# Where the first layer's q, k and v projections stand, and in which order three queues serve the first phases

## The reference, cut to what matters

```
x = x + L0_attn(layernorm(x))    # Q = rope(x Wq), K = rope(x Wk), causal; softmax of (QK + 0.1 Q^2 K^2)/sqrt(8);
                                 # a second one of the half-rotated Q, K has equal scores; gate_w on out1*out2; Wo
x = x + L0_ffn(layernorm(x))     # relu(x W1 + b1) W2 + b2, 512 wide
x = x + L1_attn(layernorm(x))    # g, b, biases on q, k, v; softmax over all positions; no output projection
x = x + L1_ffn(layernorm(x))     # (silu(x Wg) * (x Wu)) Wd, int weights / 127, 384 wide
```

## Time and profile before

| | |
|---|---|
| median of 3 runs | 368.12 us |
| profiled execution | 369.26 us |
| its span, first to last instruction | 367.5 us |
| mean granted TensorE clock | 0.944 |
| PE busy | 304.7 us (83%) |
| DVE busy | 254.1 us (69%) |
| ACT busy | 222.9 us (61%) |
| POOL busy | 168.2 us (46%) |
| DMA | 21.19 MB, mean 58 GB/s |

### The profile page before, as it was taken

How to read it: one execution, slowest core, us unless ns; L and a number is a source line. 1 busy time by engine, 2 the same in 40 slices (tenths; PEclk the granted TensorE clock), 3 DMA queues, 4 the chain that set the end, 5 groups by cost and what they waited for, 6 DMA issues and landing times.

```text
span 367.5 us, 8365 instructions
## 1 busy us (share of the span) xinstructions
PE 304.7 (83%) x2832; PEld 217.2 (59%) x2832; DVE 254.1 (69%) x993; ACT 222.9 (61%) x501; POOL 168.2 (46%) x383
## 2 busy tenths in 40 slices
PE   2862678688989997979999999989789999999654
PEld 1651556465757675757777666756556666665443
DVE  5766588787676766666767676669686989884422
ACT  5355265767566765657666766676566676767410
POOL 6253546766567575767776523515041404033020
PEclk9986668998999999999999999999999999999966
DMA  7578022423121104133101011110302010100000
GB/s 206 201 185 196 19 61 70 110 66 102 33 59 44 47 2 133 28 96 66 30 2 31 3 51 24 36 38 4 86 25 67 24 36 24 39 16 2 14 16 14
DMA packets 23034, 21.19 MB, mean 58 GB/s; under 512 B 2896, under 2 KB 20048, under 8 KB 22992
## 3 DMA queue, kind: packets, MB, share of 16 engines
q1 hardware_dynamic: 22992, 20.66, 20.7%
HBM read 13.18 MB, written 7.34 MB: 56 GB/s over the span
## 4 chain that ended last, share of the span: by engine, by line
PE 55%; DVE 16%; POOL 11%; ACT 7%; issue 5%; DMA 3%; SPq 2%; ACTq 0%; POOLq 0%
PE bank L907 11%; DVE NM L709 6%; PE bank L828 4%; PE bank L881 4%; PE bank L937 4%; PE bank L986 4%; PE bank L950 4%; DMA KS<-scr 3%; PE bank L864 3%; PE bank L978 2%; PE bank L862 2%; POOL RS L392 2%; PE bank L865 2%; DVE HG L733 2%; PE bank L814 2%
## 5 line engine op out<-in xcount | busy, mean ns | idle before, releaser
L544 ACT ACTIVATE PB<-bank 128x384 f32<-128x384 f32 (+1 forms) x256 | 136.1, 546 | 82.4 <-PE bank L883 43.8
L709 DVE TENSOR_REDUCE NM<-bank 128x2 f32<-128x512 f32 x128 | 84.9, 685 | 33.3 <-PE bank L865 33.2
L881 PE MATMUL bank<-QS,KS 128*128 128x256 f16 x256 | 70.8, 277 | 4.0 <-ACT PB L544 3.0
L907 PE MATMUL bank<-PB,VP 128*32 128x256 f32 (+1 forms) x1024 | 61.7, 359 | 1.9 <-POOL PB L431 1.2
L704 DVE CUSTOM_DVE_ANT_0 JUNK<-bank,MSF 128x128 bf16<-128x128 f32 x128 | 36.5, 285 | 38.3 <-PE bank L862 38.3
L706 DVE CUSTOM_DVE_ANT_0 JUNK<-bank,MSF 128x256 bf16<-128x256 f32 x128 | 53.7, 420 | 0.0
L907 PEld LDWEIGHTS bank<-PB,VP 128*32 128x32 f32 x1024 | 26.8, 109 | 24.9 <-issue 9.7
L431 POOL TENSOR_SCALAR_AFFINE_SELECT PB<-PB 128x512 f32<-128x512 f32 x64 | 40.6, 634 | 0.0
L458 POOL TENSOR_TENSOR xs<-xs,Y 128x256 f32<-128x256 f32 x8 | 5.8, 726 | 71.1 <-DVE Y L718 71.1
L864 PE MATMUL bank<-KS,QS 96*128 96x256 f16 x128 | 35.3, 276 | 2.9 <-DMA KS<-scr 2.9
L862 PE MATMUL bank<-KS,QS 96*128 96x256 f16 x128 | 36.2, 288 | 0.0
(11 more groups left out here) (90 smaller groups left out, 613.5 us busy)
## 6 DMA issues: line engine op xcount, KB each, us to landing
scr<-PR SPq DMA_DIRECT2D x16, 256.0 KB, 2.9
QS<-scr SPq DMA_DIRECT2D x16, 128.0 KB, 2.8
QS<-scr SPq DMA_DIRECT2D x32, 64.0 KB, 2.9
KS<-scr SPq DMA_DIRECT2D x32, 64.0 KB, 2.9
KS<-scr SPq DMA_DIRECT2D x16, 128.0 KB, 3.1
scr<-PR SPq DMA_DIRECT2D x16, 128.0 KB, 1.9
out_x<-xs SPq DMA_DIRECT2D x8, 128.0 KB, 1.9
W<-in_w SPq DMA_DIRECT2D x1, 576.0 KB, 6.1
```

Of the source, the lines that this page charges most:

```text
L544: act.activation(PB[:, s % RING, 0:n], TB_[s % 2][:, 0:n], ACT.Exp).then_inc(s_e, 1)
L709: dve.tensor_reduce(m[:, s, 0:2], o[:, :].rearrange("q (n k) -> q n k", n=2), AX.X, ALU.max, negate=True).then_inc(s_mx, 1)
L881: pe.matmul(o[:, 0:S], k[:, 0:P], q[:, :], start=True, stop=True)
L907: ins = pe.matmul(o, v, pr, start=(g % 2 == 0 and kt == 0), stop=True, skip_group_check=True)
```

## The change

The numbers of early batches and all slots of `STAGE_A` change: three batches ahead of the loop (`EARLY` = 3), batch 3 in phase -1, batch 4 from the end of phase -1 into phase 0, batch 5 in phases 0 and 1, 6 in phase 1 (statistics and norm in phase 0), 7 in phases 1 and 2, its last step in phase 3. In the straight code DVE, ACT and POOL take q and k of a batch in turn (`low` and `high` now take n), POOL clears the second ones rows after two batches' statistics and not ahead of them, and it no longer puts batch 2's statistics ahead of batch 0's sums. The scratch semaphore is split into one for q and one for k. DVE clears a piece of JUNK first, and PE multiplies it 20 times into bank 7 before its first transposes.

SP issues `store1` after the first-half loads and `load_max`. ACT copies the second half of o and the third transposed norm ahead of the slot's exponential. In phases 12 to 15 the second maxima transposes move from slot 0 to slot 1, and PE does the last pv group of the phase before ahead of them. Layer 1's down projection moves from slot 12 to 13, its addition from 13 to 14. Batch 7's layer 1 q and k projections move from slot 10 to slot 7.

```diff
-EARLY = 4
+EARLY = 3
+WARM = 20
-         "dn": (2, 12), "add_dn": (2, 13)})
-STEP_LAST0 = {... "q1": (4, 10), "qk1": (4, 10), "copy_q1": (4, 10), "copy_k1": (4, 11), ...}
+         "dn": (2, 13), "add_dn": (2, 14)})
+STEP_LAST0 = {... "q1": (4, 7), "qk1": (4, 7), "copy_q1": (4, 8), "copy_k1": (4, 8), ...}
-STAGE_A = {4: dict(bn=-16, norm=-16, xT=-15, q=-13, k=-13, v=-10, rot_q=-12, rot_k=-11, sq_q=-11, sq_k=-10, hi=-9, lo=-7),
-           5: dict(bn=-13, norm=-12, xT=-8, q=-6, k=-4, v=-3, rot_q=-5, rot_k=-3, sq_q=-4, sq_k=-2, hi=-1, lo=1),
-           6: dict(bn=-4, norm=-3, xT=1, q=3, k=3, v=6, rot_q=4, rot_k=5, sq_q=5, sq_k=6, hi=7, lo=9),
-           7: dict(bn=8, norm=9, xT=17, q=19, k=22, v=28, rot_q=20, rot_k=23, sq_q=21, sq_k=24, hi=26, lo=28)}
+STAGE_A = {3: dict(bn=-16, norm=-15, xT=-12, q=-10, k=-9, v=-8, rot_q=-9, rot_k=-8, sq_q=-8, sq_k=-7, hi=-6, lo=-5),
+           4: dict(bn=-2, norm=-1, xT=2, q=4, k=5, v=6, rot_q=6, rot_k=7, sq_q=7, sq_k=8, hi=9, lo=11),
+           5: dict(bn=4, norm=6, xT=9, q=11, k=12, v=13, rot_q=12, rot_k=14, sq_q=13, sq_k=15, hi=16, lo=17),
+           6: dict(bn=12, norm=14, xT=17, q=19, k=22, v=23, rot_q=20, rot_k=24, sq_q=21, sq_k=25, hi=26, lo=28),
+           7: dict(bn=26, norm=28, xT=30, q=33, k=42, v=44, rot_q=34, rot_k=44, sq_q=35, sq_k=45, hi=46, lo=48)}
+def m1_slot(i):
+    return 1 if phase(i - 4)[0] == 1 else 0
@@ load_stack, sync engine
-                sp.wait_ge(s_scr[L][p], 32 * (b // 2 + 1))
...
+                sp.wait_ge(s_scr[L][p][0], 16 * (b // 2 + 1))
+                ... two loads of QS
+                sp.wait_ge(s_scr[L][p][1], 16 * (b // 2 + 1))
+                ... two loads of KS
@@ sync engine's loop
-                L, b = phase(i - 4)
-                if L == 0 and b < B - 1:
-                    store1(b)
                 for (L, b), (j, place_) in LOADS.items():
                     if j == i and place_ == "mid":
                         load_stack(L, b, 0)
                 if i + 1 < NPH:
                     load_max(i + 1, 0)
-                if i == when(0, B - 1) + 4:
-                    store1(B - 1)
+                L, b = phase(i - 4)
+                if L == 0:
+                    store1(b)
@@ GpSimd
-            for b in range(EARLY):
-                rstd(0, b)
-                if b >= 2:
-                    for n in range(2):
-                        rotate(b - 2, n)
-            for b in range(EARLY - 2, EARLY):
+            for b in range(2):
+                rstd(0, b)
+            pool.wait_ge(s_rstd[0], 6)
+            ones_rows(1)
+            for n in range(2):
+                rotate(0, n)
+            rstd(0, 2)
+            for b in range(1, EARLY):
                 for n in range(2):
                     rotate(b, n)
@@ ScalarE, ahead of the loop
             for b in range(EARLY):
-                square(b, 0)
-                square(b, 1)
-                copy_v(b)
-                high(b)
+                for n in range(2):
+                    square(b, n)
+                    high(b, n)
+                copy_v(b)
@@ ScalarE's loop
+                    if s == last_pv_slot(i) + 1 and 0 <= i - 1 < NPH:
+                        evac_o(i - 1, 1)
+                    for b in due(0, "copy_xT2", i, s):
+                        ...
                     if 0 <= i < NPH:
                         exp(i, s)
-                    if s == last_pv_slot(i) + 1 and 0 <= i - 1 < NPH:
-                        evac_o(i - 1, 1)
@@ VectorE, ahead of the loop
+            dve.memset(JUNK[:, 0:2], 0.0).then_inc(s_warm, 1)
...
             variance(0, 1)
+            dve.memset(KS[0][1][0:MROW, HC:H].bitcast(U32), 0).then_inc(s_init[0][1], 1)
             normalise(1)
             dve.wait_ge(s_tab, 16)
+            product(0, 0); variance(0, 2); product(0, 1); low(0, 0); product(1, 0); low(0, 1); normalise(2)
+            product(1, 1); low(1, 0); low(1, 1); product(2, 0); product(2, 1); low(2, 0); low(2, 1)
@@ PE
+            pe.wait_ge(s_warm, 1)
+            for _ in range(WARM):
+                pe.matmul(bank[7][:, 0:S], JUNK[:, 0, 0], JUNK[:, 1, 0:2].rearrange("q n k -> q (n k)"), start=True, stop=True)
...
-                    if s == M1 and 0 <= i < NPH:
+                    if s == last_pv_slot(i) and 0 <= i - 1 < NPH:
+                        pv(i - 1, 3)
+                    if s == m1_slot(i) and 0 <= i < NPH:
                         m = into("mr1", i)
                         ...
                         max_rows(i, 1, m)
-                    if s == last_pv_slot(i) and 0 <= i - 1 < NPH:
-                        pv(i - 1, 3)
```

More of the change, by code:

```diff
@@ L107, in bank_uses @@
     for i in range(NPH):
-        uses += [(H * (i - 1) + m0_slot(i - 1), 6 if phase(i - 3)[0] == 1 else 7, ("mr0", i)), (H * i + M1, 6, ("mr1", i))]
+        uses += [(H * (i - 1) + m0_slot(i - 1), 6 if phase(i - 3)[0] == 1 else 7, ("mr0", i)), (H * i + m1_slot(i), 6, ("mr1", i))]
         L, b = ORDER[i]
@@ L220, in program @@
         s_hi, s_lo = sem("hi_0"), sem("lo_0")
-        s_scr = [[sem(f"scratch_{L}{p}") for p in range(2)] for L in range(2)]
+        s_scr = [[[sem(f"scratch_{L}{p}{n}") for n in range(2)] for p in range(2)] for L in range(2)]
         s_hi1, s_lo1 = sem("hi_1"), sem("lo_1")
@@ L307, in load_stack @@
                     sp.wait_ge(s_t, H * when(L, b - 2) + HC * (c + 1))
[L308 removed]
                 sq, sk = [scr[L][b:b + 1, n].rearrange("o s (d h) t -> (o s d) h t", h=H) for n in range(2)]
[L310 to L312 removed]
+                sp.wait_ge(s_scr[L][p][0], 16 * (b // 2 + 1))
+                sp.dma_start(QS[L][p][0:R, cs], sq[:, cs]).then_inc(s_st[L][p][c], 16)
+                sp.dma_start(QS[L][p][R:R + h, cs], sq[0:h, cs]).then_inc(s_st[L][p][c], 16)
+                sp.wait_ge(s_scr[L][p][1], 16 * (b // 2 + 1))
+                sp.dma_start(KS[L][p][0:h, cs], sk[0:h, cs]).then_inc(s_st[L][p][c], 16)
+                sp.dma_start(KS[L][p][h:h + R, cs], sk[:, cs]).then_inc(s_st[L][p][c], 16)
             def store0(b):
@@ L379, in _, with ones_rows @@
             pool.wait_ge(s_eps, 3)
-            for p in range(2):
+            def ones_rows(p):
                 pool.memset(KS[0][p][MROW:P].bitcast(U32), TWO_ONES).then_inc(s_ones[0], 1)
                 pool.wait_ge(s_ones[0], p + 1)
+            ones_rows(0)
             def rstd(n, b):
@@ L515, in copy_v, with high @@
                 act.copy(va_(b), halves(psum("v0", b))).then_inc(*empties("v0", b))
-            def high(b):
+            def high(b, n):
                 p = b % 2
                 if b >= 2:
[L520 to L523, removed]
+                    act.wait_ge(s_scr[0][p][n], 16 * (b // 2))
+                act.wait_ge(s_sq, 2 * b + n + 1)
+                act.copy(PR[p][:, n, 0:2], QR[p][:, n]).then_inc(s_hi, 1)
             clear(QS[0][0][:, :, :], s_init[0][0])
@@ L599, in _ @@
                         if b >= 2:
-                            act.wait_ge(s_scr[1][b % 2], 32 * (b // 2))
+                            for n in range(2):
+                                act.wait_ge(s_scr[1][b % 2][n], 16 * (b // 2))
                         act.wait_ge(*emptied("qk1", b))
@@ L661, in product, with low @@
                 dve.tensor_tensor(TQ[p][:, n], psum(name, b)[:, :], TAB[:, n], ALU.mult).then_inc(*empties(name, b))
-            def low(b):
+            def low(b, n):
                 p = b % 2
-                for n in range(2):
-                    dve.wait_ge(s_hi, 2 * b + n + 1)
-                    dve.tensor_tensor(PR[p][:, n, 2:4], QR[p][:, n], PR[p][:, n, 0:2], ALU.subtract).then_inc(s_lo, 1)
+                dve.wait_ge(s_hi, 2 * b + n + 1)
+                dve.tensor_tensor(PR[p][:, n, 2:4], QR[p][:, n], PR[p][:, n, 0:2], ALU.subtract).then_inc(s_lo, 1)
             dve.wait_ge(s_x[0], 16)
@@ L674, in _ @@
             variance(0, 1)
+            dve.memset(KS[0][1][0:MROW, HC:H].bitcast(U32), 0).then_inc(s_init[0][1], 1)
             normalise(1)
-            dve.memset(KS[0][1][0:MROW, HC:H].bitcast(U32), 0).then_inc(s_init[0][1], 1)
             dve.wait_ge(s_tab, 16)
-            for n in range(2):
-                product(0, n)
+            product(0, 0)
             dve.wait_ge(s_x[2], 16)
             variance(0, 2)
+            product(0, 1)
+            low(0, 0)
+            product(1, 0)
+            low(0, 1)
             normalise(2)
-            for n in range(2):
-                product(1, n)
-            low(0)
-            variance(0, 3)
-            normalise(3)
+            product(1, 1)
+            low(1, 0)
+            low(1, 1)
             for n in range(2):
                 product(2, n)
-            low(1)
             for n in range(2):
-                product(3, n)
-            low(2)
-            low(3)
+                low(2, n)
             dve.wait_ge(s_msf, 16)
@@ L779, in _ @@
                         if a["lo"] == H * i + s:
-                            low(b)
+                            for n in range(2):
```

(1 more changed line is left out.)

19 lines of the change are left out of this document (9 added, 10 removed).

## The result

| | before | changed |
|---|---|---|
| median | 368.55 us (4 runs, 367.98 to 369.64) | 355.32 us (4 runs, 354.21 to 356.15) |
| ratio, 95% interval | 1 | 0.9636 [0.9597, 0.9674] |
| profiled execution, its span | 369.26, 367.5 | 354.21, 352.5 |
| mean granted clock | 0.944 | 0.935 |

Forecast were 344.5 us, range 336 to 355, and a speed-up with 0.95. The sign was right; the time lies just outside the range.

The account below looks back on a forecast made before the run. Half-idle engines bound the start, hand-overs phases 0 and 1, PE from phase 3. Terms -8.0 - 7.5 + 3.5 - 5.0 - 4.7 - 2.0 = -23.7 took the profiled 369.26 to 345.6 us, median 344.5; range 336 to 355.

Parts of the forecast that it names:

- The start, -8.0: Up to VectorE's first maximum: three batches instead of four, 23.2 us instead of 31.16; bounds -6.5 and -9.5.
- The 0.9 us for the clear beside the normalisation: In the start: GpSimd's 1.8 us clear beside VectorE's second normalisation costs 0 to 1.8 us, taken as 0.9.
- The filler's gain on the projection: In the start: if fillers warm the clock, batch 0's projection goes from 3.75 towards 1.99 us; up to 1.8 reaches the chain.
- The stretch up to phase 0, -7.5: First maximum to first exponential: one batch instead of two, 16 us instead of 23.30; bounds -5 and -9.
- Phases 0 to 3, +3.5: Layer 0's first phases take over two batches: 19.1, 18.9, 18.9, 17.9, sum 74.8 against 71.6 us; bounds 0 and +10.
- the 82 that the prediction had named as the sign of being wrong: Phases 0 to 3: the prediction called itself wrong if they take over 82 us.
- three slots lie between a normalisation and its transposes: Moved batches' slots: three between normalisation and transposes, given as the argument against the rival "Given back in phases 0 to 2".
- The sync queue, -5.0: Layer 1's store goes behind the stack load and maxima's row: four PE waits of 6.0 us go; bounds -6 and -2.
- ScalarE's order, -4.7: Copies of o and third norm ahead of the exponential: PE's 3.5 + 3.2 us of waits can go; bounds -6.7 and 0.
- Layer 1's end, -2.0: From phase 12, later maxima transposes and down projection shrink PE's waits at phase starts, over four phases; bounds -4 and 0.
- The tail, 0: After 330 us: a chain in which no order changes, so 0.
- Given back in phases 0 to 2: Rival, chance 0.18: in-order engines stop at hand-overs, as PE did at 34.89; moved batches cost +10, not +3.5: 351 us.

Follow-up runs that it names:

- e12: e1 with the second ones rows cleared by GpSimd behind batch 1's sums, not beside VectorE's second normalisation: 349.25 us, ratio 0.9501.
- e1: Changed kernel with batch 7's layer 0 statistics, norm and transposes at slots 23, 25, 28 instead of 26, 28, 30: 351.74 us, ratio 0.9558.
- e9: e1 with batch 7's k projection at slot 34 and v at 38 instead of 42 and 44, last steps at 44 and 46: 350.24 us.
- e17: e16 plus eight fillers ahead of PE's wait for each of three second norms, batch 7's last subtractions at slot 49, not 46: 344.95 us.
- e14: e12 with four 16-bit filler matmuls of 256 columns in every slot ahead of phase 0: 347.21 us, ratio 0.9435.
- e7: Changed kernel with 30 filler matmuls (16-bit, 256 columns) ahead of PE's wait for batch 7's norm: 353.46 us, ratio 0.9597.
- e2: Kernel before with only layer 1's store moved behind the first-half loads and the maxima's row in the sync queue: 360.96 us, ratio 0.9817.
- e3: Kernel before with only ScalarE's copies of o (second half) and third transposed norm ahead of the slot's exponential: 364.50 us, ratio 0.9914.
- e4: Kernel before with only layer 1's later slots: second maxima transposes behind the last pv group, down projection and addition one slot later: 366.22 us.
- e6: Changed kernel with sync queue order, ScalarE's order and layer 1's slots as before; start, filler and layer 0 projection slots stay: 365.97 us.
- e15: e12 with VectorE's RoPE product of every batch of the loop one slot after PE's projection, not in the same slot: 348.85 us, ratio 0.9480.
- e16: e9 and e12 in one kernel, with e14's fillers in the slots ahead of phase 0: 348.63 us, ratio 0.9473.
- e8: Changed kernel with both ones rows cleared by GpSimd ahead of the first statistics again: 355.36 us, ratio 0.9655.

## Why the forecast missed, step by step

- *The start, -8.0.* Right, -8.1: first maximum at 23.10 for a forecast of 23.2. The 0.9 us for the clear beside the normalisation was a little small (1.4 on the normalisation, 1.2 on the first maximum, e12). The filler's gain on the projection did not reach the first maximum (23.11 in e1 with 3.47 us).
- *The stretch up to phase 0, -7.5.* Right, -7.9; first exponential at 38.49 for 39. Both rest on an execution in which the clock fell as it did; others of the changed kernel take up to 2 us more.
- *Phases 0 to 3, +3.5.* The step that failed: +13.4, outside even its bound of +10, and 85.05 us, over the 82 that the prediction had named as the sign of being wrong. It was built as a sum of busy times with a margin of 1.2 to 3 us of idle over the fullest engine (its four terms add to 74.8, which is +3.2; for the other 0.3 it gives no row). Phase 1 came at 22.4 for 18.9: two normalisations in one slot, which the loop of GpSimd and the slot numbers show (`norm1` at 16 + 12, batch 7 at 28). I had written that three slots lie between a normalisation and its transposes; for batch 7 it is two, and I had not laid the moved steps beside the steps that stay. At the full clock and without the collision phase 1 takes 18.0 to 18.8 us (e1, e9, e17), what was forecast. Phase 0 came at 20.4 for 19.1: 1.1 us of it is the clock (19.29 in e14). Phase 2 came at 23.7 for 18.9: 1.8 us of low clock, left by the stop (e7), 1.7 us of order within the phase (e9, where phase 3 took it back, and e17, where it did not), and 1.35 us of mis-sized terms: at the full clock e9's phase 2 has PE busy for 18.3 us where the sum had 17.8, and 1.9 us of idle where it left 1.1. Phase 3 came at 18.6 for 17.9, with a clock of 0.91 where 1.00 had been.
- *The sync queue, -5.0, and ScalarE's order, -4.7.* Right in sum by luck: alone the queue gives 6.7 us and ScalarE's order 3.2, 9.9 for 9.7, one 1.7 over and one 1.5 under. The queue's bound of 6 was PE's wait; the phases with a late load shorten by 6.5 us in e2's profile, nearer to the 6.9 of PEld's waits. The -11.8 us of phases 4 to 11 hold more than these two: in the profiles e2 gives 6.6 us there, e3 2.5, e4 0.8 and e6 1.9, the last two of which the forecast did not have there.
- *Layer 1's end, -2.0.* Right in mechanism and size: -1.9 in the profile, in three phases, -1.5 alone.
- *The tail, 0.* +1.1: some 0.6 of low clock, and 0.4 that come with layer 1's later slots (e4).
- *The rivals.* "Given back in phases 0 to 2" is what happened, by the mechanism named (an engine in order stops at another's late hand-over, as at 34.89), but at 355 and not 351: it had +10 for phases 0 to 3, with no term for the clock that a stop leaves behind. Its 0.18 was too low; the range ended 0.3 us short.
- What stays open: why a front costs 4 to 6 us in a phase that PE fills and 3 in good slots. e15 does not settle whether VectorE's wait for the product has a part in it, and no run separates the queues of ScalarE and GpSimd. Open too is why the clock fell in phase 1 of e12 and e14 and not of e1.

## What to carry to other kernels

When steps are moved in a schedule that several engines walk in order, write down for each slot what every engine already has there: a sum of busy times cannot see that two pieces are due at once, and one stop of 4 us cost 3.7 to 6.2 us of two phases, with the low clock behind it, and some 3 us of the kernel. Work on the queue order of late loads first; it was the smallest edit and gave half the gain. A stall on PE can have two prices, the stop and the low clock after it; filler matmuls kept the clock up in the phases behind them in e7, e14 and e17, but not in e16, and e7's gain is not clear of noise.

## What the hardware showed that I had not expected

- A GpSimd clear, which only writes, stretched two VectorE tensor_scalar instructions from 0.60 us (e12) to 1.97: they began 0.02 us ahead of the clear of 1.80 us and ended 0.15 behind it. The Trainium skill (SBUF — State Buffer, Who interferes with whom) describes the port pair that VectorE and GpSimd share as an exclusive lock; the rows agree, for a writer too.
- The clock's low stretches fall differently in executions of nearly the same kernel: phase 0 took 20.4 us in the changed kernel, 22.2 in e1 and 21.1 in e12, which have the same instructions in it, at clocks of 0.86, 0.79 and 0.84, and 19.29 in e14 and e17 at 1.00. The 20 fillers of the start gave batch 0 the high clock in 11 of 14 profiles (1.97 us) and not in three (3.47 to 3.75: e1, e8, e9).
